# A grouped convolution with normalised input on one core: sums taken later, one inverse root on ACT, taps copied by GpSimd, first and last units normalised by two engines

## What is computed

```python
def _gn(v, G=32, eps=1e-5):
    B_, C_, H_, W_ = v.shape
    g = v.reshape(B_, G, C_ // G, H_, W_)
    m = jnp.mean(g, axis=(2, 3, 4), keepdims=True)
    s = jnp.var(g, axis=(2, 3, 4), keepdims=True)
    return ((g - m) / jnp.sqrt(s + eps)).reshape(v.shape)

x_cat = jnp.concatenate([v, v[:, :, :-1, :]], axis=2)        # v = _gn(x)
out = lax.conv_general_dilated(x_cat, weight, (1, 1), 'VALID', feature_group_count=384)
return x + out + bias[None, :, None, None]
```

## Time and profile before

| | |
|---|---|
| median of 3 runs | 794.35 us (793.08 to 794.4) |
| the profiled execution, its own time | 795.17 us |
| its span, first to last instruction | 793.4 us |
| PE, PEld | 683.9 us (86%), 563.7 us (71%) |
| DVE | 676.0 us (85%) |
| ACT | 704.1 us (89%) |
| POOL | 607.6 us (77%) |
| DMA | 319.47 MB, mean 403 GB/s |

### The profile page before, as it was taken

One profiled execution on the slowest core, in us unless ns is written; L12 is line 12 of the kernel. 1 busy time (PEld: TensorE's weight loads), 2 busy tenths in 40 slices (PEclk: granted clock), 3 DMA queues, 4 the chain that ended last, 5 costly groups with the idle time before them and its releaser, 6 DMA issues.

```text
span 793.4 us, 9149 instructions
## 1 busy us (share of the span) xinstructions
PE 683.9 (86%) x1920; PEld 563.7 (71%) x1920; DVE 676.0 (85%) x1538; ACT 704.1 (89%) x1093; POOL 607.6 (77%) x1174
## 2 busy tenths in 40 slices
PE   0499999988898888898888898989989998999996
PEld 0377877776787776686776686867767776777775
DVE  6899999888889888889888889888898888898852
ACT  7699999998889898899898898989889898898993
POOL 4588888877787777787778786778778787786885
PEclk9999999999999999999999999999999999999998
DMA  8979999999999999999999999999999999999855
GB/s 351 409 308 387 419 425 428 425 427 426 426 428 427 427 423 424 403 414 405 427 423 424 407 399 426 414 425 373 425 428 400 426 419 422 407 402 427 371 233 249
DMA packets 41224, 319.47 MB, mean 403 GB/s; under 512 B 12304, under 2 KB 12432, under 8 KB 12432
## 3 DMA queue, kind: packets, MB, share of 16 engines
q1 hardware_dynamic: 41168, 318.89, 97.3%
HBM read 164.70 MB, written 154.14 MB: 402 GB/s over the span
## 4 chain that ended last, share of the span: by engine, by line
DMA 34%; PE 17%; POOL 12%; ACT 11%; DVE 9%; SPq 8%; issue 8%; POOLq 0%; ACTq 0%
DMA xt_even<-first 22%; PE conv L491 15%; DMA xt_odd<-seconds 7%; ACT xn L406 6%; DVE st L341 6%; SPq L213 4%; POOL xt_odd L298 4%; ACT kept L421 4%; SPq L198 4%; POOL xt_even L298 3%; DVE xt_odd L358 2%; DMA out<-xt_even 2%; DMA out<-xt_odd 2%; DMA xt_even<-wide_first 1%; POOL newt L285 1%
## 5 line engine op out<-in xcount | busy, mean ns | idle before, releaser
L491 PE MATMUL conv<-xn,runs 128*128 128x448 f32 x1536 | 653.2, 573 | 58.8 <-issue 37.2
L491 PEld LDWEIGHTS conv<-xn,runs 128*128 128x128 f32 x1536 | 514.3, 346 | 127.6 <-issue 76.7
L341 DVE BATCH_NORM_STATS2 st<-xt_even 128x6 f32<-128x336 f32 x512 | 225.9, 495 | 53.4 <-DMA xt_even<-first 48.4
L298 POOL TENSOR_TENSOR xt_even<-xt_even,kept 128x448 f32<-128x448 f32 x192 | 218.7, 1139 | 67.4 <-ACT kept L421 67.4
L406 ACT ACTIVATE xn<-xt_even,shift,rstd 128x672 f32<-128x672 f32 x256 | 231.8, 945 | 22.3 <-POOL shift L287 22.3
L421 ACT ACTIVATE kept<-conv,bias_all 128x448 f32<-128x448 f32 x384 | 237.9, 624 | 14.5 <-PE conv L491 12.1
L341 DVE BATCH_NORM_STATS2 st<-xt_odd 128x6 f32<-128x336 f32 x512 | 226.1, 494 | 27.6 <-DMA xt_odd<-seconds 27.6
L298 POOL TENSOR_TENSOR xt_odd<-xt_odd,kept 128x448 f32<-128x448 f32 x192 | 218.5, 1138 | 25.6 <-ACT kept L421 25.6
L406 ACT ACTIVATE xn<-xt_odd,shift,rstd 128x672 f32<-128x672 f32 x256 | 231.6, 942 | 0.1
L358 DVE SCALAR_TENSOR_TENSOR xt_even<-conv,bias_all,xt_even 128x448 f32<-128x448 f32 x192 | 128.8, 671 | 14.3 <-PE conv L491 13.7
L358 DVE SCALAR_TENSOR_TENSOR xt_odd<-conv,bias_all,xt_odd 128x448 f32<-128x448 f32 x192 | 128.6, 670 | 11.9 <-PE conv L491 11.7
(11 more groups left out here) (34 smaller groups left out, 180.1 us busy)
## 6 DMA issues: line engine op xcount, KB each, us to landing
xt_odd<-seconds SPq DMA_DIRECT2D x64, 672.0 KB, 7.8
out<-xt_even SPq DMA_DIRECT2D x64, 672.0 KB, 6.8
out<-xt_odd SPq DMA_DIRECT2D x64, 672.0 KB, 6.7
xt_even<-first SPq DMA_DIRECT2D x32, 768.0 KB, 7.5
xt_even<-first SPq DMA_DIRECT2D x32, 744.0 KB, 7.7
xt_odd<-seconds SPq DMA_DIRECT2D x64, 336.0 KB, 8.7
out<-xt_even SPq DMA_DIRECT2D x64, 336.0 KB, 7.8
out<-xt_odd SPq DMA_DIRECT2D x64, 336.0 KB, 7.3
```

What stands on the lines that cost most here:

```text
L298: nc.gpsimd.tensor_tensor(cell, cell, kept_of(u, c), ALU.add).then_inc(pool_added, 1)
L341: ins = nc.vector.bn_stats(st[:, n % RS, h, b, :], x_of(n)[:, h, b * ROW:(b + 1) * ROW])
L491: nc.tensor.matmul(bank(c), lay[:, :, c], channel_of(xn[:, u % NS, :, :], c), start=True, stop=True).then_inc(conv_ready, 1)
```

## The change

**Sums later.** `LATE = 4`: in unit u DVE first takes the last four pieces of statistics of unit u + 2 and then the first twelve of unit u + 3. POOL's `add_means` of unit u + 2 moves from the end of unit u - 1 (k = 4) to unit u (k = 0), and with it every step of the chain: the tables `USUAL` and `SPECIAL` name the place of each. In a usual unit `mean` stands after PE's channel 5 (before: 2), `variance` after channel 8 (5), `negmean` at ACT's k = 2 (1), `deviations` at POOL's k = 1 (0), `newton` at POOL's k = 2 (3). `root` stays at ACT's k = 3, and `add_vars` goes from behind DVE's k = 3 to before its k = 4.

**The inverse root.** ACT computes it in one instruction, and DVE's `invert` is gone. The Newton step stays. Both programs have two table loads on ACT, both ahead of the first unit:

```diff
-                nc.scalar.activation(std[:, n % RS, :], var[:, n % RS, :], ACT.Sqrt, bias=eps[:, 0:1]
-                                     ).then_inc(std_ready, 1)
+                nc.scalar.activation(r0[:, n % RS, :], var[:, n % RS, :], ACT.Abs_reciprocal_sqrt, bias=eps[:, 0:1]
+                                     ).then_inc(r0_ready, 1)
```

**The taps.** POOL makes all four copies, now in the even unit (u = 2, 4, ... for the group after u's), behind its adds k = 3 and k = 4. It waits for its own add ahead of each pair and for the copies behind it:

```diff
-                pool.wait_ge(x_loaded[u % XS][h], 16 * len(PIECES) * (u // XS + 1))
-                nc.gpsimd.tensor_copy(taps_place(g, 0, h), taps_source(g, 0, h)).then_inc(taps_laid, 1)
+                for h in range(HALVES):
+                    pool.wait_ge(x_loaded[u % XS][h], 16 * len(PIECES) * (u // XS + 1))
+                    nc.gpsimd.tensor_copy(taps_place(g, par, h), taps_source(g, par, h)).then_inc(taps_laid, 1)
+                pool.wait_ge(taps_laid, COPIES * g + HALVES * (par + 1))
...
+                    if u % PER_GROUP == 0 and 0 < u < UNITS - PER_GROUP and k in (3, 4):
+                        pool.wait_ge(pool_added, through(ACT_CH, u, c))
+                        lay_out(u // PER_GROUP + 1, k - 3)
```

**Two engines normalise five units.** Of units 0, 1 and 2 (`POOL_HELPED`) POOL normalises three of the eight batches, of units 62 and 63 (`DVE_HELPED`) DVE does. PE's first convolution of such a unit waits for both:

```diff
+            def normalize(n, b):
+                pool.wait_ge(coef_ready, n + 1)
...
+                nc.gpsimd.tensor_scalar(xn[:, n % NS, :, part], x_of(n, part), rstd[:, n % RS, b:b + 1],
+                                        shift[:, n % RS, b:b + 1], ALU.mult, ALU.add).then_inc(pool_normed, 1)
...
+                    if u + LEAD_NORM in DVE_HELPED and k == 0:
+                        normalize(u + LEAD_NORM, ACT_BATCHES, BP)
```

**The start.** The memset of slot 5 on POOL stands ahead of the first sums (before: behind the third). PE does `variance(1)` after the second convolution of unit 0 (before: ahead of the first). Taps of groups 0 and 1 are copied before unit 0. DVE's statistics of units 0 and 1 follow a table of their own, 19 pieces in each:

```diff
-            ends = (3, 6, 8, 11, 13, 16)
+            ends = (0, 3, 6, 8, 11, 13, 16)
+            at_start = ((38, 42, 45, 48, 51, 54, 57), (57, 61, 65, 68, 71, 74, 76))
             for u in range(UNITS):
+                begin = (u + LEAD_STATS) * ALL - LATE
+                parts = at_start[u] if u < len(at_start) else [begin + e for e in ends]
```

176 lines of the change are left out of this document (89 added, 87 removed).

## The result

The change takes 807.0 us (median of four runs, 805.2 to 808.55), the kernel before 794.38 beside it (793.08 to 795.91): the ratio is 1.0154, 95% interval 1.0134 to 1.0174. It is slower by 1.5%, 12.6 us, where I forecast 787.0. The profiled execution took 805.2 us, the shortest of the four; its span is 803.4.

The account below looks back on a forecast made before the run. The DMA queue, busy 97.3% of the span, was taken as the bound, then its slow stretches. From 795.2 us, 5 (middle), 1.5 (start) and 1 (end) gave 787.7, less 0.8: 787.0 us; range 779 to 796.

Parts of the forecast that it names:

- The middle, 5 us gained: Middle of the run: later sums bring three of four load requests 2 to 2.4 us sooner; 5 us gained.
- The queue is longer by about that at most times. I take 5 us of the 11.8: Middle: requests 2 to 2.4 us sooner lengthen the DMA queue, recovering 5 of 11.8 us lost against 426 GB/s.
- a queue that runs dry on some of its engines: Second half of the run: supposed cause of the slow stretches, 414 GB/s instead of 426 from 320 to 740 us.
- the DMA is at its own limit: Rival, middle: slow stretches belong to the memory, not a short queue; start and end may cancel, 794 us; chance 0.15.
- my sign of 7 us: Near 600 us: 336 KB stores landing after 7 us or more would show the forecast right.
- The queue's ring: Middle: from the second half's landing to the store's issue, 5.7 us in odd units and 7.7 in even ones.
- it fits, with little left: POOL in even units: adds, Newton, deviations, sums and the added copies take 11.5 of 11.7 us.
- The slower rival: Middle: POOL becomes the bound, its even unit above 11.7 us; at 12.0, 0.1 us a unit more, 800 us; chance 0.16.
- The start, 1.5 gained: First units: earlier first convolution and stores plus earlier memset of slot 5; 1.5 us gained, between 2 lost and 6 gained.
- the third and fourth as before, the fifth about 1 us later: Start: times of the third to fifth stores; the fifth later since unit 3's coefficients stand at unit 1's end.
- The end, 1 gained: Last units: DVE's help saves PE's one wait for xn, 0.5 us; 1 us gained in all, between 0 and 3.
- The inverse root needs no further table: ACT, all 64 units: rival that the inverse root needs another table set, paying loads each unit; given no chance.

Follow-up runs that it names:

- e6: The kernel before with the inverse root and the change's later places of statistics, sums, mean, variance and root; copies, start and end as before: 799.82 us, ratio 1.0061.
- e11: The change with POOL's two sums of odd units ahead of its first add, from unit 3 on: 808.03 us, ratio 1.0162.
- e5: The kernel before with all tap copies from the third group on made by POOL in even units: two executions 800.73 and 800.84 us, four 840 to 852.
- e3: The change with the start of the kernel before, including the prologue and copies of groups 0 and 1: 802.81 us, ratio 1.0088.
- e12: The kernel before with the inverse root on ACT and three of eight batches of the last two units normalised by DVE: 795.35 us, ratio 1.0009.
- e4: The kernel before with one inverse root on ACT in place of ACT's root and DVE's reciprocal, nothing else: 796.44 us, ratio 1.0012.
- e1: The change with tap copies of groups 2 and on back in the odd unit, side 0 on POOL, side 1 on ACT: 806.39 us, ratio 1.0131.
- e13: The change with four matmuls of constants ahead of the mean in odd units, their bias awaited only in unit 3: 805.11 us, ratio 1.0103.
- e7: The change without its end: DVE normalises nothing and unit 61 has the usual places: 804.12 us, ratio 1.0106.
- e15: The kernel before with the inverse root, slot 5 zeroed early, POOL normalising three batches of unit 0, unit 2's coefficients kept early: 790.26 us, ratio 0.9933.

## Why the prediction was wrong, step by step

All three terms of the sum came out with the other sign. By the moved bytes the middle lost 1.8 us (4.6 to 300 us, 2.8 back) where I had 5 gained, the start 5.8 where I had 1.5 gained, the end 2.4 where I had 1 gained.

*The middle, 5 us gained.* The step that failed is "The queue is longer by about that at most times. I take 5 us of the 11.8". The late order alone (e6) has DVE waiting less (37.2 us for even loads, 48.4 before) and a queue about 1 us longer up to 200 us, where nothing was to be gained. In the slow half it is longer for the last piece of a store only, and the rate is 413 GB/s where it was 414: 0 us gained. The step before it, which I called least sure, "a queue that runs dry on some of its engines", is not settled. For it speaks that large pieces land after 6 to 7 us there while small ones still take 12 to 14. Against it, that the busy share does not fall in the dips. The share alone decides nothing, since the change, paced by its own ring, also shows 1.01 at 415 to 417 GB/s and dips in both halves. So the rival "the DMA is at its own limit" is neither shown nor excluded: the kernels whose chain has 29% or more of DMA fall from 423 to 426 GB/s to 409 to 416 behind 320 us, whatever their order. My was one store of 4.9 us, and the median of 580 to 660 us is 6.5 (6.7 in the change, which has 8.4 for the one in 594 to 600), so my sign of 7 us did not come. "DMA: Bandwidth & Descriptors" in the Trainium skill, section "Where 436 GB/s comes from", puts the bound at about 358, half of what it gives for a stack that two cores share, and the traces of this one core disagree: 426 over 200 us and more in seven kernels.

*The queue's ring.* This part was right: I gave 7.7 us from landing to store in even units, e11 shows 7.9. In odd units, where I gave 5.7, e11 has 6.7 (landing 603.72, store 610.45). But in the change it is not the ring that binds.

*POOL's even unit, "it fits, with little left".* The unit takes POOL 12.35 us (133.62 to 145.97 in the change, 0.59 of it a wait for ACT), more than the 11.5 I summed. Two units still fit: in the round at full clock they take it 22.7 us. What I left out is who stands behind it. In TensorE's order a `mean` that waits for POOL holds back six channels, their banks, ACT and DVE, and then POOL itself. The slower rival named this chain (mean for the even unit's copies, ACT for mean, root for ACT) and put its price at 0.1 us a unit; it was (23.90 - 23.4)/2 = 0.25 on average until 300 us. Its condition, an even unit of POOL above 11.7 us, was met and does not decide: at full clock the round is 22.69 us all the same. And no step of mine had TensorE's clock. Its fall behind a wait is 1.6 us in 20 of 27 rounds here, and 39 us and more between two executions of e5.

*The start, 1.5 gained.* To the first store every number held: `shift` 21.02 (21.3), PE at 25.61 (26.0), ACT's first batch of unit 1 at 31.48 (31.51), store 39.29 (39.4). The batch on POOL took 907 ns, between my 0.75 and the 1.0 that "GPSIMD Engine Reference" of the Trainium skill, section 3.1, would give; the trace is nearer to the page. The second store came 2.8 us sooner (44.56 for 47.40), as I gave it. What failed is "the third and fourth as before, the fifth about 1 us later": they came 2.45, 2.55 and 4.25 us later. I counted ACT's batches and not what `mean` and `variance` of unit 2 do between TensorE's units. By e3 the start costs 3.7 us by the bytes at 49.8 MB and 5.2 in time, against a lower bound of 2.

*The end, 1 gained.* Helping is worth nothing measurable (e12); I had given it 0.5 us. The mean of unit 63 came later by more than my 0.7 us: it waited 4.13 us, and the end lost 2.4. The late order alone, with the usual place, lost 3.8 there (e6), so the special place is not the whole cause.

*The inverse root needs no further table.* Right (the rival had no chance); and the root gains nothing measurable (e4).

The range (779 to 796) left no room for a start and a ring that both lose. Both go back to something that I had in the order of the instructions and did not price: a matmul pair whose input POOL delivers late, placed ahead of convolutions that need nothing from it, and the clock behind its wait.

What stays open: what makes the dips of the DMA and the uneven landings from 320 us on, and how much of e1's, e11's and e13's gain at 300 us was lost to that and how much to longer rings (their spans scatter by 5 us). Of the end only sizes are known, 2.4 us by the bytes and 0.5% by e7, and not how much of it is the late order's.

## What to carry to other kernels

Before a step moves, write down for each in-order engine what stands behind the waiting instruction; a small matmul that waits for another engine holds up the whole pipeline, not only its own 0.4 us. Where the steady pace is set by a queue, spend the work on what comes ahead of it: the 4.8 us by which e15 stored its first two units sooner were nearly all there at the end (4.3 in the profiled executions), while the 5 us that e11 won by 300 us were not. And when helpers share a start, keep the later units' coefficients ahead of the convolutions, as e15 does.
